# A graph layer pair on one core: strips of four known blocks, a tail of twelve, and the preparations in other places

## What is computed

```python
deg = sum(adj, axis=1) + 1
h_neigh = (adj @ x + x) / deg
z = relu(concat([x, h_neigh]) @ W0 + b0)
x1 = layernorm(x + z / norm(z))                 # first layer, row by row
neigh = (adj @ x1) / deg
out = layernorm(x1 + concat([x1, neigh]) @ W1.T)  # second layer
```

## Time and profile before

| | us |
|---|---|
| median of 3 runs | 761.63 (760.83 to 764.16) |
| profiled execution | 762.74 |
| its span, first to last instruction | 760.9 |
| TensorE products busy | 630.8 (83%) |
| VectorE busy | 682.1 (90%) |
| ScalarE busy | 588.8 (77%) |
| GpSimd busy | 312.3 (41%) |
| mean DMA rate over the span | 361 GB/s |
| mean granted TensorE clock | 0.948 |

### The profile page before, as it was taken

One profiled execution on the slowest core, in us unless ns is written; L12 is line 12 of the kernel. 1 busy time (PEld: TensorE's weight loads), 2 busy tenths in 40 slices (PEclk: granted clock), 3 DMA queues, 4 the chain that ended last, 5 costly groups with the idle time before them and its releaser, 6 DMA issues.

```text
span 760.9 us, 27768 instructions
## 1 busy us (share of the span) xinstructions
PE 630.8 (83%) x11125; PEld 580.0 (76%) x11125; DVE 682.1 (90%) x2506; ACT 588.8 (77%) x815; POOL 312.3 (41%) x360
## 2 busy tenths in 40 slices
PE   1357687687777778979899998999999999998994
PEld 0246677676776677878788887989898989988994
DVE  4499998989998999899999999999999999987895
ACT  1978879989898888989889898888898888850021
POOL 0233323433421425664354545556553546341025
PEclk9987877989999997999999999999999999999998
DMA  9999999999999999999999999999999999900003
GB/s 361 406 366 402 420 347 420 422 420 418 421 419 419 419 419 407 382 419 419 419 414 420 408 421 402 420 413 408 413 391 420 399 418 394 420 24 2 2 18 102
DMA packets 41516, 274.54 MB, mean 361 GB/s; under 512 B 4455, under 2 KB 8615, under 8 KB 8615
## 3 DMA queue, kind: packets, MB, share of 16 engines
q1 hardware_dynamic: 39040, 270.55, 87.1%
q10 hardware_dynamic: 2342, 2.16, 0.9%
HBM read 270.60 MB, written 2.10 MB: 358 GB/s over the span
## 4 chain that ended last, share of the span: by engine, by line
PE 31%; DVE 25%; issue 13%; ACT 11%; DMA 11%; POOL 7%; ACTq 2%; DVEq 0%; POOLq 0%; SPq 0%
PE s_ps L385 17%; DMA a_in<-in_adj 11%; ACT junk L589 8%; DVE e L802 7%; DVE t_sb L809 6%; PE u_ps L404 5%; POOL small L1179 4%; PE p_ps L371 2%; PE z_ps L454 2%; DVE q_sb L870 2%; DVE y_sb L864 2%; ACTq L577 2%; PE p_ps L466 1%; DVE a_in L809 1%; POOL store L1211 1%
## 5 line engine op out<-in xcount | busy, mean ns | idle before, releaser
L589 ACT ACTIVATE junk<-a_in 128x2048 uint8<-128x2048 uint16 x256 | 488.4, 1913 | 8.8 <-DMA a_in<-in_adj 8.6
L385 PE MATMUL s_ps<-xh,t_sb 128*128 128x129 f16 x4096 | 388.2, 251 | 52.3 <-DVE t_sb L809 48.8
L385 PEld LDWEIGHTS s_ps<-xh,t_sb 128*128 128x128 fp8e4 x4096 | 314.7, 103 | 81.3 <-DVE t_sb L809 53.8
L802 DVE TENSOR_SCALAR e<-a_in 128x2048 uint8<-128x2048 f32 x256 | 314.1, 1234 | 18.7 <-DMA a_in<-in_adj 17.9
L1211 POOL COPY store<-pk 128x32 uint32<-128x32 uint32 (+1 forms) x250 | 176.1, 746 | 179.9 <-ACT pk L598 179.9
L809 DVE TENSOR_SCALAR t_sb<-pk 128x128 uint32<-128x128 uint32 x1024 | 159.1, 227 | 5.6 <-ACT pk L598 4.8
L371 PE MATMUL p_ps<-pow_h,e 128*128 128x16 f16 x2048 | 90.8, 171 | 65.7 <-DVE e L802 55.0
L371 PEld LDWEIGHTS p_ps<-pow_h,e 128*128 128x128 f16 x2048 | 77.6, 99 | 79.9 <-DVE e L802 60.1
L1179 POOL TENSOR_TENSOR small<-small,minus_half 128x4 f32<-128x4 f32 x32 | 68.8, 2150 | 151.8 <-DVE small L858 104.9
L404 PE MATMUL u_ps<-xh,u_sb 128*128 128x64 f16 x2976 | 105.6, 192 | 0.0
L404 PEld LDWEIGHTS u_ps<-xh,u_sb 128*128 128x128 fp8e4 x2976 | 100.6, 97 | 1.2
(11 more groups left out here) (119 smaller groups left out, 487.5 us busy)
## 6 DMA issues: line engine op xcount, KB each, us to landing
a_in<-in_adj SPq DMA_DIRECT2D x256, 1024.0 KB, 11.2
xl<-in_x ACTq DMA_DIRECT2D x4, 512.0 KB, 18.3
out_h<-e SPq DMA_DIRECT2D x8, 256.0 KB, 2.1
b_sb<-in_L_gnn_b ACTq DMA_DIRECT2D x3, 0.2 KB
w_sb<-in_L_gnn_W ACTq DMA_DIRECT2D x1, 32.0 KB
w_raw<-in_L_gnn_W ACTq DMA_DIRECT2D x1, 32.0 KB
```

The source lines that it names most:

```text
L385: last = nc.tensor.matmul(s_ps[:, n % 2, at:GW], t_sb[:, b // 2, b % 2::2], xh[:, b, at:GW], start=(b == 0), stop=False)
L589: nc.scalar.activation(junk[:, t % 2, :], halves[t % R], ACT.Copy, scale=1.0 / 128, accum_out=half_sum[:, n, c:c + 1]).then_inc(s_half, 1)
L802: nc.vector.tensor_scalar(e8[:, c, :], a_in[:, t % R, :], 1.0, float(CODE), ALU.is_equal, ALU.add).then_inc(s_e, 1)
```

## The change

Segments now have four turns and strips four blocks (the first strip has eight, the last segment eight turns). A known block's sums go in as two products, g high with 64 columns and g low with x in 193 columns, with both g parts falling on the same 64 columns of the result; `agg` gets 193 columns for 257. The join of g is thereby gone, the join of x is on VectorE in `mean`. The tail has 12 blocks, from 52: passes 0 to 7 take eight of them, passes 8 to 15 take four, all with products of 64 columns and one add. The buffers of the passes with four blocks are separate, so they can be unpacked early; those of the passes with eight are two in place of six. x goes on SyncE's queue behind the chunks of row block 0, and `split_x`, `weights`, `bias` and `guard_x` change places.

```diff
-START = [0, 12, 20, 28, 36, 44, 52]
+START = [0, *range(12, 60, 4)]
+W2 = 4
+SW = F + XW
+GUARD = [20, 24, 28, 32]
-VR = 6
+VR = 2
...
@@ SyncE, in the loop over n
+                if n == 0:
+                    for q in range(NC):
+                        sp.dma_start(x_in[:, q * CB:(q + 1) * CB, :].rearrange("p (j r) f -> p j (r f)", r=IL),
+                                     x_j[:, q * CB // IL:(q + 1) * CB // IL, :]).then_inc(s_x[q], 16)
...
@@ TensorE, sum_quarter
-                    at = 0 if b < lows(n) else HP
-                    last = nc.tensor.matmul(s_ps[:, n % 2, at:GW], t_sb[:, b // 2, b % 2::2], xh[:, b, at:GW],
-                                            start=(b == 0), stop=False)
+                    row_bits = t_sb[:, b // 2, b % 2::2]
+                    if b < lows(n):
+                        nc.tensor.matmul(s_ps[:, n % 2, 0:F], row_bits, g_hi[:, b, :], start=(b == 0), stop=False)
+                    if 0 < b < lows(n):
+                        last = nc.tensor.matmul(s_ps[:, n % 2, 0:SW], row_bits, xh[:, b, F:GW], start=False, stop=False)
+                        continue
...
@@ ScalarE
-            for q in range(NC):
-                act.dma_start(x_in[:, q * CB:(q + 1) * CB, :].rearrange("p (j r) f -> p j (r f)", r=IL),
-                              x_j[:, q * CB // IL:(q + 1) * CB // IL, :]).then_inc(s_x[q], 16)
+            act.wait_ge(s_const, 1)
+            nc.scalar.copy(warm[:, :], ident[:, 0:1])
...
@@ VectorE, mean
-                dve.wait_ge(s_xsum, e + 1)
+                hi, lo = (agg[:, par, :, F + i * F:2 * F + i * F] for i in range(2))
+                link(nc.vector.tensor_tensor(hi, hi, lo, ALU.add))
...
@@ VectorE, the loop over n
+                if n == 1:
+                    for q in range(NC):
+                        split_x(q)
                 compare(n, 0)
...
+                if n == 0:
+                    bias()
...
                 if n == 1:
                     weights()
-                    bias()
-                if 3 <= n < 7:
-                    guard_x(n - 3)
+                if n in GUARD:
+                    guard_x(GUARD.index(n))
...
@@ VectorE, the tail
             mean(e)
+            unpack_tail(NV)
+            add_tail(0)
             unpack_tail(2)
+            norm(e)
+            unpack_tail(NV + 1)
+            add_tail(1)
             unpack_tail(3)
...
@@ GpSimd
-            def join_x(e):
+            def keep_degrees(e):
```

More of the change, by code:

```diff
@@ L69, with kept @@
 TAIL = low(NQ - 1)
-WIDTH = [W] * (NQ - 1) + [NB - TAIL]
-ROWS = [START[s + 1] - 1 for s in range(NQ - 1)] + [NB]
-BASE = [sum(ROWS[t] * WIDTH[t] * PKW for t in range(s)) for s in range(NQ + 1)]
+WIDTH = [low(s + 1) - low(s) for s in range(NQ - 1)]
+ROWS = [START[s + 1] - 1 for s in range(NQ - 1)]
+KEPT = [(i * W, W) for i in range(6)] + [(6 * W, NB - 6 * W)]
+KEPT_ROWS = [max(ROWS[s] for s in range(NQ - 1) if at <= low(s) < at + w) for at, w in KEPT[:-1]] + [NB]
+NK = len(KEPT)
+BASE = [sum(KEPT_ROWS[t] * KEPT[t][1] * PKW for t in range(s)) for s in range(NK + 1)]
+def kept(block):
+    return max(i for i in range(NK) if KEPT[i][0] <= block)
 def piece(slot):
@@ L80, in piece @@
     return j * ROWS[q - 1] // steps, (j + 1) * ROWS[q - 1] // steps
-PIECE = max(piece(n)[1] - piece(n)[0] for n in range(START[1], NB))
+PIECE = max((piece(n)[1] - piece(n)[0]) * WIDTH[seg(n) - 1] for n in range(START[1], NB))
 def turn(slot):
@@ L266, in stored, with stored_blocks, tail_unit @@
         def stored(s, row, rows):
-            w = WIDTH[s] * PKW
+            w = KEPT[s][1] * PKW
             return store[:, BASE[s] + row * w:BASE[s] + (row + rows) * w]
+        def stored_blocks(first, blocks, row, rows):
+            s = kept(first)
+            at = (first - KEPT[s][0]) // 2
+            return stored(s, row, rows).rearrange("p (r u w) -> p r u w", r=rows, w=2 * PKW)[:, :, at:at + blocks // 2, :]
+        def tail_unit(j):
+            if j < NV:
+                size = TG * W // 2
+                return v_sb[:, (j % VR) * size:(j % VR + 1) * size, :]
+            size = TG * W2 // 2
+            at = VR * TG * W // 2 + (j - NV) * size
+            return v_sb[:, at:at + size, :]
         def lows(n):
@@ L399, in catch_up @@
                         pe.wait_ge(s_uadd, turn(n))
[L400 removed]
+                half, w = (r1 - r0 + 1) // 2, WIDTH[q - 1]
                 for r in (range(half), range(half, r1 - r0))[half_of]:
[L402 removed]
+                    for b in range(w):
                         for part in range(2):
[L404 removed]
+                            last = nc.tensor.matmul(u_rows[:, r, 0:F], u_sb[:, (r * w + b) // 2, b % 2::2],
                                                     xh[:, low(q - 1) + b, part * F:(part + 1) * F],
[L406 removed]
+                                                    start=(b + part == 0), stop=(b + part == w))
                     if r == r1 - r0 - 1:
@@ L988, in _ @@
                 e, k = n // BR - 1, n % BR
+                if n == 1:
+                    for q in range(NC):
+                        split_x(q)
                 compare(n, 0)
-                if n == 1:
-                    split_x(0)
                 if n:
@@ L1236, in _ @@
                 e, k = n // BR - 1, n % BR
-                if e >= 0 and k == 1:
-                    join_x(e)
                 if e >= 0 and k == 2:
@@ L1250, in _ @@
             own_rows(NE - 1)
-            join_x(NE - 1)
-            join_g(NE - 1)
+            keep_degrees(NE - 1)
             root(0, NE - 1)
```

142 lines of the change are left out of this document (59 added, 83 removed).

## The result

| | changed | before, beside it |
|---|---|---|
| median, first comparison | 779.7 us (774.1 to 786.4, 4 runs) | 762.6 us |
| ratio, 95% interval | 1.020 (1.013 to 1.027) | |
| median, second comparison | 776.5 us (771.9 to 779.9, 4 runs) | 762.1 us |
| ratio, 95% interval | 1.017 (1.012 to 1.022) | |

The change made the kernel 14 to 15 us slower. The forecast was 764.3 with 756 to 770.5: too low, and the time is outside the range. The execution of 786.4 us in the first comparison counts as a slow one, so the ratio leaves it out (the other three have a median of 777.6) and its profile is not read.

What follows compares the result with a forecast made beforehand. It took DMA to bound the kernel up to 460 us, TensorE rows 44 to 63, then a tail of TensorE passes beside a chain. Terms -1.2 + 6.9 - 3.0 = +2.7 on 761.6 gave 764.3 us, range 756 to 770.5.

Steps and rivals of the forecast that it cites:

- the split product: TensorE, known blocks as 64 and 193 columns: 114 ns in place of 112, 0.1 us a row of 48.
- The Trainium skill's price: Added TensorE load and product pairs at about 81 ns: near 48 us for the last twenty rows, some 812 us; chance 0.01.
- Lag at row 43: VectorE over the 40.0 us DMA line in rows 20 to 43: 9.0 us, between 5.4 and 12.6.
- Rows 44 to 63: Rows bound by TensorE, with denser pieces and the split: +6.9 us together, between +5.5 and +9.
- The term for the pieces: TensorE in rows 52 to 55: 102 products a turn for 68, 1.0 us; with the split, group +4.5 us (45.8).
- Start: First 120 us: moved x, bias, weights and guards take back 7 of 7.5 us lost from DMA.
- the second term: DMA from 120 to 460 us, 416 GB/s against 420: the 3.2 us lost there are regained.
- Tail: After the stream: verdict() ends 1.5 us earlier, the step to variance(3) shrinks 1.5: -3.0, between -1.5 and -6.
- Rival 2: Clearly slower: VectorE's waits stay, long adds hold up compare in rows 48 to 55: +9.1, 770.7 us; chance 0.32.
- Rivals 1, 3 and 4: 1: guards, pieces vanish in slack, 757.3, 0.19; 3: tail's thirteen us in full, 754.0, 0.04; 4: start gives nothing, 771.3, 0.04.

Runs made afterwards that it cites:

- d1_prep_seg4: Kernel before with preparations moved and segments and strips of four blocks; one product of 257 columns, joins on GpSimd, tail of sixteen: 761.6 us, ratio 0.998.
- e1_strips_apart: a2_onemm with a place of its own in the store for each strip of four blocks: 767.4 us, ratio 1.005.
- a2_onemm: Changed kernel with a known block as one product of 257 columns again and the joins of g and x on GpSimd again: 769.0 us, ratio 1.010.
- a1_again: The changed kernel itself, unaltered, run for a second profile: 776.5 us, ratio 1.017 to the kernel before.
- c7_split_light: b5_split with only half the columns of each chunk transferred from row 44 on: 764.6 us, ratio 1.002.
- b5_split: Kernel before with only the split product (64 and 193 columns), join of g gone, join of x on VectorE: 775.9 us, ratio 1.018.
- b4_prep: Kernel before with only the moved preparations, x on SyncE, guards at rows 20, 24, 28 and 32: 759.5 us, ratio 0.997.
- c9_even: a2_onemm with the pieces cut at even rows: 766.5 us, ratio 1.005.
- e2_after_light: Changed kernel with only half the columns of each chunk transferred from row 44 on: 773.8 us, ratio 1.014.
- c10_guards: b4_prep with guards at rows 8, 12, 16 and 40 in place of 20, 24, 28 and 32: 759.9 us, ratio 0.995.

## Why the prediction was wrong

By medians the pieces add up, each less the kernel before of its comparison: preparations and segments -1.5 (d1_prep_seg4), with the tail of twelve +4.7 (e1_strips_apart), with the strips side by side +6.9 (a2_onemm), with the split +14.4 (a1_again). By the profiles the forecast misses by 14.5 (+17.2 for +2.7): 8.3 up to turn 43, 6.7 in turns 44 to 63, -0.5 in the tail.

**The step that failed is the split product** ("0.1 us a row of 48 known blocks, 0.25 if each adds 5 ns"). As TensorE work it was sized about right: 0.14 a row in c7_split_light, and between 700.16 and 703.07 of a1_again 25 such pairs take 116 ns each, forecast 114. What it put at nothing is the supply of instructions. The split adds 1,753 products and as many loads to the changed kernel's list, 1,637 to that of b5_split, and the list comes 256 at a time. With the chunk transfers beside it a packet can come after TensorE has used up the last one. The split costs 13.9 us in the kernel before, and 11.3 of them go when the transfers are halved. In the changed kernel it costs 7.6 by the medians; the late packets of turns 44 to 63 are 5.0 by the profiles, and the next paragraph has what came before them. The forecast counted columns and never asked how fast the instructions come. The Trainium skill's price that it weighed (TensorE: Matmul & The Clock Gate, Back-to-back issue gap: about 81 ns for a pair of 128 columns) was rightly set aside: even 64 and 193 columns together take 116 ns, not twice 81.

**Lag at row 43.** Forecast 9.0 us, row 43 at -1.2; measured +7.1. Without the split it is +1.7, near the forecast, but partly by luck, since two misses pull against each other: the start gained about 5 in place of 10.2 (b4_prep), and the lag against b4_prep, which has the guards too, is 6.7 in place of 9.0. The odd unpacks do not show in it (c9_even +1.9). The other 5.4 came with the split, in turns 24 to 35, where stops without a releaser are few. There VectorE is late, TensorE waits, and the granted clock falls soon after a wait: TensorE's first product after its wait for a compare, and windows of 1 us,

```profile
335.63 0.36 PE L404 MATMUL p_ps<-pow_h,e 128*128 128x16 f16 x8 [1.65 <-DVE e L838]
```

```profile
335.00:336.00 1.00, 0.36 (x8) 0.27 (x8) 1.00 (x5) 1.00 (x3) 1.00 (x1) 0.92 0.90 377
336.00:337.00 1.00, 0.29 (x5) 0.29 (x6) 0.92 (x7) 1.00 (x1) 0.70 (x1) 0.50 1.03 410
...
341.00:342.00 1.00, 1.00 (x17) 0.96 (x16) 1.00 (x3) 0.78 (x2) 0.00 (x0) 0.50 1.03 426
342.00:343.00 1.00, 1.00 (x15) 0.96 (x13) 1.00 (x9) 1.00 (x1) 0.00 (x0) 0.66 1.05 385
```

TensorE's wait of 1.65 us ends at 335.63, and from 335.9 on the clock stands at its lower level (0.50, 1.2 GHz) for 6.8 us, although TensorE is busy without a pause at the end of them. The three groups of turns 24 to 35 have a mean clock of 0.88 to 0.89 in a1_again and 0.92 to 1.00 in a2_onemm. That the changed kernel has more of these spells with the split than without is seen; that they are what costs the 5.4, and why the split brings them, is not shown and stays open.

**Rows 44 to 63.** Forecast +6.9, between 5.5 and 9. Measured +13.6; with packets in time (e2_after_light) +8.6, and +7.2 with one product. The term for the pieces was right (45.6 us for turns 52 to 55, forecast 45.8); 5.0 of the missing 6.7 are the late packets. The run with the segments alone and the pair d1_prep_seg4 and e1_strips_apart show what the forecast blurred: not the strips of four, but the tail of twelve brings this cost.

**Start.** -7 and -3.2 were forecast; b4_prep shows -8.9 at turn 7 and about -5 from turn 19 on, the medians -2.6. Its first two windows, with the columns of the earlier trace rows, tell the two terms apart:

```profile
0.00:120.00 120.00, 74.42 (x980) 66.92 (x981) 93.05 (x277) 97.57 (x127) 28.84 (x80) 0.80 1.00 408
120.00:460.00 340.00, 283.16 (x4810) 255.98 (x4807) 323.97 (x1226) 299.02 (x409) 162.18 (x208) 0.94 1.01 413
```

408 GB/s for 385 is (408 - 385)/420 x 120 = 6.6 us, near the 7. But 413 for 416 means that the 3.2 us after 120 us did not come back; (416 - 413)/420 x 340 = 2.4 us more went. So the second term failed. That the four guards took it is refuted by c10_guards, which moves 413 GB/s there too; what takes it was not found.

**Tail.** Forecast -3.0, measured 20.7 to 17.2, -3.5. VectorE's timeline has the first operation of verdict(), the add behind it and two variances:

```profile
744.83 0.28 DVE L999 TENSOR_SCALAR u_sb<-half_sum 128x256 f32<-128x256 f32 x1
...
749.02 0.69 DVE L962 TENSOR_TENSOR xl<-s_ps,xl 128x512 f32<-128x512 f32 x1
...
760.01 0.69 DVE L968 TENSOR_REDUCE fvar<-t_sb 128x8 f32<-128x512 f32 x1 [1.54 <-ACT t_sb L692]
...
762.80 0.69 DVE L968 TENSOR_REDUCE fvar<-t_sb 128x8 f32<-128x512 f32 x1 [0.70 <-ACT t_sb L692]
```

The first pass starts at 707.29, so verdict() ends 41.7 us behind it, before 729.51 - 686.11 = 43.4: 1.7 earlier, forecast 1.5. The variance at 760.01 comes 11.0 behind that, before 13.2, forecast 11.7. The steps of 2.8 stayed. From the first pass to the last TensorE is busy for 51.8 us in place of 63.2, 11.4 less (forecast 13.3); the tail of twelve gives 3.5 of them, and costs 9 in turns 52 to 63.

**The rivals.** Rival 2 (clearly slower, 770.7) had the sign, and its mark, TensorE idle for over 2 us in a group of rows 48 to 55, came in one of the two. Its mechanism, TensorE waiting for a compare, shows in turns 28 to 35, but not where the rival had put it: of the 2.3 us in which TensorE is idle in turns 52 to 55, the three stops above are 1.8. Rivals 1, 3 and 4 did not come.

## What to carry to other kernels

Before splitting an operation in two because the columns come out equal, count instructions: work out how long the engine takes for 256 of them while DMA is full (here stops came at 5.8 to 6.4 us and none at 6.9 or more), and look for stops marked "issue" in the middle of unbroken work, a packet apart. A shorter tail is paid for in the loop: compare the microseconds off the last chain (3.5) with those put on the rows that are bound (9). And test parts alone: strips of four looked guilty and cost nothing in the end, the "free" split cost the most.

## What the runs showed of the hardware

- TensorE's list came in packets of 16,384 bytes, one for 127 loads and 127 products. With chunks at 382 to 424 GB/s, stops of 0.2 to 1.6 us (a1_again and b5_split) ended 2.2 to 2.6 us after a packet started; with half the transfers the stops behind row 44 were gone.
- It is no fixed rate: 130 products and 128 loads ran in 4.4 us at 400 GB/s without a stop. From turn 40 on, stops came where 254 recorded instructions lasted 5.8 to 6.4 us on average over a group, none where they lasted 6.9 and more.
- In the tail, where DMA is all but idle, 128 pairs of 64 columns take 3.83 us and pass follows pass, and q8's packets start 3.8 to 4.0 us apart (736.1 to 751.6 in a1_again).
- An unpack of eleven rows of sixteen words in a strided layout took 325 ns for 245 in a contiguous one.
- 0.3 us behind a wait of TensorE of 1.65 us the clock fell to its lower level for 6.8 us.
